# Graph network on one core: propagation started by nine buckets, six row places, and scattered records laid out so that gates load as whole records

## What is computed

```python
# 0: relations. h2 = relu(x @ W1[r] + b1) @ W2[r] for 8 relations
x = ln(x + relu(segment_sum(h2[src, rel_type] * norm, dst) + bias2))
# 1: attention. a = softmax of edge_weight1 within each dst
x = ln(x + elu(segment_sum(x[src] * a[:, None], dst)))
# 2: propagation, twice, over the edges and a loop at each node: r = src, c = dst
w = dinv[r] * dinv[c]                      # dinv = rsqrt(degree)
for _ in range(2):
    y = segment_sum(w[:, None] * y[c], r)  # y = x at first
x = ln(x + y)
# 3: gated messages. gate = silu(edge_attr @ W1.T + b1) @ W2.T + b2 + adapt(src, dst)
agg = segment_sum(gate * x[dst] * (cw * mj)[:, None], src) / clip(segment_sum(mj, src))
x = ln(x + ln(x + agg) * gamma + beta)     # the layer has a layernorm of its own
```

## Time and profile before

| | us |
|---|---|
| three runs: median (lowest to highest) | 6699.7 (6696.94 to 6712.73) |
| the profiled execution, its own time | 6714.21 |
| span of its trace, first to last instruction | 6711.9 |
| busy in the span: PE / DVE / ACT / POOL | 3883.5 / 4094.4 / 2565.0 / 3959.9 |

### The profile page before, as it was taken

How to read it: one execution, slowest core, us unless ns; L and a number is a source line. 1 busy time by engine, 2 the same in 40 slices (tenths; PEclk the granted TensorE clock), 3 DMA queues, 4 the chain that set the end, 5 groups by cost and what they waited for, 6 DMA issues and landing times.

```text
span 6711.9 us, 121393 instructions
## 1 busy us (share of the span) xinstructions
PE 3883.5 (58%) x46613; PEld 2995.6 (45%) x46613; DVE 4094.4 (61%) x7196; ACT 2565.0 (38%) x5259; POOL 3959.9 (59%) x3993
## 2 busy tenths in 40 slices
PE   5445555555555555345555655555565555798775
PEld 5344444333332333224444444444444444787774
DVE  4444444555555556436656666666666667888999
ACT  1111111111111111234445555455455556787664
POOL 2566666666666666665555555555555554236996
PEclk8555555555555555555555555555555556899998
DMA  3455422222222222123333323333333333587886
GB/s 125 157 172 163 136 50 50 48 57 48 49 48 49 48 49 51 30 44 56 58 55 56 59 61 59 56 57 58 57 61 57 58 57 70 159 231 190 190 193 132
DMA packets 1408683, 571.24 MB, mean 85 GB/s; under 512 B 1063555, under 2 KB 1347727, under 8 KB 1407969
## 3 DMA queue, kind: packets, MB, share of 16 engines
q1 hardware_dynamic: 1303201, 452.37, 30.1%
q0 software_dynamic: 104896, 110.96, 7.5%
HBM read 394.81 MB, written 168.16 MB: 84 GB/s over the span
## 4 chain that ended last, share of the span: by engine, by line
PE 22%; another core or an unknown queue 22%; issue 17%; ACT 14%; DVE 14%; DMA 7%; SPq 2%; POOL 2%; DVEq 0%; ACTq 0%; POOLq 0%
DMA rb<-dst_rows 5%; PE ps L1314 4%; PE ps L1527 4%; ACT rb L1674 3%; ACT meta_b L1684 3%; DVE ps L2167 2%; PE ps L1352 2%; ACT meta_a L1606 2%; PE ps L1485 2%; ACT at_table L1704 2%; ACT rb L1704 1%; PE ps L1274 1%; ACT meta_b L1691 1%; PE ps L1302 1%
## 5 line engine op out<-in xcount | busy, mean ns | idle before, releaser
L992 POOL DMA_INDIRECT by_src<-meta_a,row_src x1612 | 1609.0, 998 | 1280.5 <-DVE meta_a L2422 863.7
L981 POOL DMA_INDIRECT ring<-h_table,meta_b x1616 | 1647.4, 1019 | 900.5 <-issue 448.6
L1591 ACT ACTIVATE ring<-ring,meta_b 128x48 f32<-128x48 f32 x1616 | 386.3, 322 | 2103.0 <-DMA ring<-h_table,meta_b 2070.3
L1485 PE MATMUL ps<-dst_i,meta_b 128*128 128x128 bf16 x2450 | 393.4, 292 | 834.1 <-ACT at_table L1704 291.6
L1314 PE MATMUL ps<-ring,WX 128*128 128x48 bf16 x2188 | 437.5, 236 | 554.0 <-DVE row_src L2298 340.7
L2661 DVE TENSOR_TENSOR meta_b<-big,ps 128x1152 bf16<-128x1152 bf16 x546 | 734.6, 1346 | 0.0
L1485 PEld LDWEIGHTS ps<-dst_i,meta_b 128*128 128x128 bf16 x2450 | 228.6, 151 | 1062.4 <-issue 1035.1
L1444 PE MATMUL ps<-WX,meta_b 128*128 128x49 bf16 (+1 forms) x14742 | 594.6, 200 | 77.1 <-issue 43.2
L1314 PEld LDWEIGHTS ps<-ring,WX 128*128 128x128 bf16 x2188 | 361.1, 165 | 581.4 <-DVE row_src L2298 351.8
L1314 PE MATMUL ps<-row_src,WX 128*128 128x48 bf16 x4376 | 490.9, 234 | 220.5 <-issue 218.4
L1444 PEld LDWEIGHTS ps<-WX,meta_b 128*128 128x128 bf16 (+1 forms) x14742 | 574.9, 108 | 93.1 <-issue 46.3
(11 more groups left out here) (353 smaller groups left out, 9089.3 us busy)
## 6 DMA issues: line engine op xcount, KB each, us to landing
by_src<-default SPq DMA_DIRECT2D x44, 1456.0 KB
meta_a<-by_src SPq DMA_DIRECT2D x273, 216.0 KB, 4.3
rb<-lo_rows SPq DMA_DIRECT2D x202, 256.0 KB
rb<-src_rows SPq DMA_DIRECT2D x273, 144.0 KB
rb<-dst_rows SPq DMA_DIRECT2D x273, 144.0 KB
meta_a<-in_attrT SPq DMA_DIRECT2D x402, 80.0 KB
ring<-h_table,meta_b POOLq DMA_INDIRECT x1616
by_src<-meta_a,row_src POOLq DMA_INDIRECT x1612
```

Of the source, the lines that this page charges most:

```text
L981: pool.indirect_dma_start(ring[:, gg % RING, j, 0:width], None, table, bass.IndirectOffsetOnAxis(ap=index(g * GROUP + j), axis=0)) \
L992: pool.indirect_dma_start(by_src, bass.IndirectOffsetOnAxis(ap=row_src[:, t:t + 1], axis=0), rec[:, q % RECS, j, :], None).then_inc(s_sc[q ...
L1485: mm = pe.matmul(bank(5, P, at=i * P), ohS_n[:, a % 3, :, u * TRIO + i], ohK_n[:, a % 2, u * TRIO + i, :], start=True, stop=True)
L1591: scaled = act.activation(row, row, ACT.Copy, scale=meta_b[:, t, M_NORM:M_NORM + 1])
```

## The change

Four edits.

1. *Place of a record.* `place_cells` now works out (128 s + place) x 50 + j: the 50 cells of one place of a source bucket are neighbours, and the 128 places of a cell lie 10,400 bytes apart. The fetches of the fields follow it.
2. *Gates as whole records.* The nine cells of a group then are one run of 9 x 208 = 1,872 bytes on each of the 128 partitions. The load takes the whole records (`gate_n` grows from 48 to 52 floats a record) and is cut where a group passes from one source bucket to the next (`pieces`).
3. *Six row places.* `rb_8` has six slots for the last layer (the three above it served as slots of block stores until then), with semaphores of their own (`s_rowl`). The first six rows are loaded ahead of propagation, before the block loads from the seventh on; row n+6 is loaded right behind the gates of group n, once row n has been turned.
4. *Propagation begun with nine buckets.* DVE works out dinv right after the degrees, scales and splits chunk 0 (nine buckets) and goes into the loop over blocks; the other chunks and the attention of the last four buckets are steps taken in that loop, two before an even block and one before an odd one. ACT answers the exponential at block 19 and the square root at block 27. PE waits in group 0 for the chunk when it comes to the chunk's first bucket.

```diff
@@ place_cells
-                link(dve.tensor_scalar(count_i, dst_i[:, :], 7, 7, ALU.logical_shift_right, ALU.logical_shift_left))
-                link(dve.scalar_tensor_tensor(rows_f, bucket[:, :], float(PER_SRC * P), scratch, ALU.mult, ALU.add))
-                link(dve.tensor_tensor(rows_f, rows_f, count_i, ALU.add))
+                link(dve.tensor_scalar(count_i, dst_i[:, :], 7, None, ALU.logical_shift_right))
+                link(dve.scalar_tensor_tensor(rows_f, bucket[:, :], float(P), scratch, ALU.mult, ALU.add))
+                link(dve.scalar_tensor_tensor(rows_f, rows_f, float(PER_SRC), count_i, ALU.mult, ALU.add))
...
@@ SP: fetches of the fields
-            by_cell = by_src.rearrange("(t p) w -> p t w", p=P)
-            by_bucket = by_src[0:CELLS * P, :].rearrange("(s j p) w -> p s j w", j=PER_SRC, p=P)
+            by_bucket = by_src[0:CELLS * P, :].rearrange("(s p j) w -> p s j w", j=PER_SRC, p=P)
+            after_cells = by_src[CELLS * P:CTILES * P, :].rearrange("(p j) w -> p j w", p=P)
-                by_tile = by_src[0:CELLS * P, :].rearrange("(s j p) w -> j s p w", j=PER_SRC, p=P)
+                by_tile = by_src[0:CELLS * P, :].rearrange("(s p j) w -> j s p w", j=PER_SRC, p=P)
@@ SP: before the block loads, and the last layer
+            def last_rows_load(n):
+                if n >= STORES:
+                    sp.wait_ge(*turned(SGROUPS + n - STORES))
+                    sp.wait_ge(*last_rows_in(n - STORES))
+                sp.dma_start(rb_8[:, n % STORES, :], dst_rows[n * SG:(n + 1) * SG, :].rearrange("(a t) n -> a (t n)", a=1)
+                             .to_broadcast([P, SG * P])).then_inc(s_rowl[n % STORES], 16)
+            sp.wait_ge(*turned(SGROUPS - 1))
+            for n in range(STORES):
+                last_rows_load(n)
             for l in range(LOADS_AHEAD, len(LOADS)):
...
-            for m in range(SGROUPS, 2 * SGROUPS):
-                n = m - SGROUPS
-                sp.wait_ge(*turned(m - 3))
-                sp.wait_ge(s_rowd[m % 3], 16 * (m // 3))
...
-                sp.dma_start(gate_n[:, n % 4, :, :], by_cell[:, n * SG:(n + 1) * SG, 0:FEAT]).then_inc(s_gld[n % 4], 16)
+            for n in range(SGROUPS):
                 if n >= 4:
+                    sp.wait_ge(*gates_in(n - 4))
                 sp.wait_ge(s_msg, SGROUPS + n - 3)
+                for s, j0, j1, at in pieces(n):
+                    sp.dma_start(gate_n[:, n % 4, at:at + j1 - j0, :], by_bucket[:, s, j0:j1, :]).then_inc(s_gld[n % 4], 16)
...
+                if n + STORES < SGROUPS:
+                    last_rows_load(n + STORES)
@@ PE
+                        if k == 0 and c == 0 and d in STARTS:
+                            pe.wait_ge(s_xp, 2 + STARTS.index(d))
...
-                pe.wait_ge(s_xp, 2)
+                pe.wait_ge(s_nacc, N_BUCKETS)
+                pe.wait_ge(s_msg, SGROUPS)
@@ ACT
-                answer("exp", elu[:, 0:LATE[1] - LATE[0], :])
-                answer("sqrt", small[:, 3, LATE[0]:LATE[1]])
                 for b in range(N_BLOCKS):
+                    if b == LATE_EXP_AT:
+                        answer("exp", elu[:, 0:LATE[1] - LATE[0], :])
+                    if b == LATE_ROOT_AT:
+                        answer("sqrt", small[:, 3, LATE[0]:LATE[1]])
@@ DVE
-                late = [attend_chunk(*LATE)]
-                steps(late, 2)
-                inverse_degree()
-                steps(late, 1000)
+                def scaled_chunk(c):
+                    a, b = STARTS[c], CHUNK_ENDS[c]
+                    v, q = V[:, a:b, :], Q[:, a:b, :]
+                    part = [XP[:, a:b, i * FEAT:(i + 1) * FEAT] for i in range(PARTS)]
+                    link(dve.tensor_tensor(v, X[:, a:b, :], dinv[:, a:b][:, :, None].to_broadcast([P, b - a, FEAT]), ALU.mult))
+                    yield
+                    link(dve.tensor_copy(part[0], v))
+                    yield
+                    link(dve.tensor_tensor(q, v, part[0], ALU.subtract))
+                    yield
+                    link(dve.tensor_copy(part[1], q))
+                    yield
+                    link(dve.tensor_tensor(q, q, part[1], ALU.subtract))
+                    yield
+                    dve.tensor_copy(part[2], q).then_inc(s_xp, 1)
+                    yield
...
                 split_multiplicities()
-                link(dve.tensor_tensor(V[:, :, :], X[:, :, :], bc(dinv[:, :]), ALU.mult))
-                for _ in split_steps(V[:, :, :], s_xp):
-                    pass
-                dve.wait_ge(s_xp, 2)
+                inverse_degree()
+                dve.wait_ge(s_dinv, 1)
+                queue = [scaled_chunk(0)]
+                steps(queue, 1000)
+                queue = [scaled_chunk(c) for c in range(1, SUPERS - 1)] + [attend_chunk(*LATE), scaled_chunk(SUPERS - 1)]
                 for b in range(N_BLOCKS):
                     k, c, _, ns, d, own = block_of(b)
+                    if b < STARTS[-1]:
+                        steps(queue, 2 if b % 2 == 0 else 1)
```

More of the change, by code:

```diff
@@ L492, in pieces, with gates_in @@
                 yield d, t0 - d * PER_SRC, t1 - d * PER_SRC, t0 - a0
+        def gates_in(n):
+            return s_gld[n % 4], 16 * sum(len(list(pieces(x))) + (x == SGROUPS - 1 and CTILES > CELLS)
+                                          for x in range(n % 4, n + 1, 4))
         def stored(a):
@@ L497, in stored, with last_rows_in @@
             return BLKW[i] + 16 * sum(len(list(pieces(x))) for x in range(i, a + 1, STORES))
+        def last_rows_in(n):
+            i = n % STORES
+            return s_rowl[i], stored((SGROUPS - 1 - i) // STORES * STORES + i) + 16 * (n // STORES + 1)
+        assert STORES == 6
         SUPERS = len(STARTS)
@@ L588, in build @@
         EXP_IN, ROOT_IN = 3, 14
+        LATE_EXP_AT, LATE_ROOT_AT = 19, 27
         SUMS_AT, NORM_STEPS, ROOT_AT = 5, (13, 19, 25), 21
@@ L913, in _ @@
                 sp.wait_ge(s_blkw[a % STORES], stored(a))
+            for i in range(2):
+                sp.wait_ge(s_roww[i], 48 * len(range(i, N_BUCKETS, 2)))
+            sp.wait_ge(s_padw, 32)
+            def last_rows_load(n):
[7 more added lines that the diff above has]
+                last_rows_load(n)
             for l in range(LOADS_AHEAD, len(LOADS)):
@@ L918, in _ @@
                 block_load(l)
-            for m in range(SGROUPS, 2 * SGROUPS):
-                n = m - SGROUPS
-                sp.wait_ge(*turned(m - 3))
-                sp.wait_ge(s_rowd[m % 3], 16 * (m // 3))
-                if n == 0:
-                    for i in range(2):
-                        sp.wait_ge(s_roww[i], 48 * len(range(i, N_BUCKETS, 2)))
-                    sp.wait_ge(s_padw, 32)
-                sp.dma_start(rb_8[:, m % 3, :], dst_rows[n * SG:(n + 1) * SG, :].rearrange("(a t) n -> a (t n)", a=1)
-                             .to_broadcast([P, SG * P])).then_inc(s_rowd[m % 3], 16)
+            for n in range(SGROUPS):
                 if n >= 4:
-                    sp.wait_ge(s_gld[n % 4], 16 * (n // 4))
+                    sp.wait_ge(*gates_in(n - 4))
                 sp.wait_ge(s_msg, SGROUPS + n - 3)
-                sp.dma_start(gate_n[:, n % 4, :, :], by_cell[:, n * SG:(n + 1) * SG, 0:FEAT]).then_inc(s_gld[n % 4], 16)
+                for s, j0, j1, at in pieces(n):
+                    sp.dma_start(gate_n[:, n % 4, at:at + j1 - j0, :], by_bucket[:, s, j0:j1, :]).then_inc(s_gld[n % 4], 16)
+                if n == SGROUPS - 1 and CTILES > CELLS:
+                    sp.dma_start(gate_n[:, n % 4, SG - (CTILES - CELLS):SG, :], after_cells).then_inc(s_gld[n % 4], 16)
+                if n + STORES < SGROUPS:
+                    last_rows_load(n + STORES)
             sp.wait_ge(s_tab, 1)
@@ L1687, in turn_at_once @@
                 def turn_at_once(m):
-                    act.wait_ge(s_rowd[m % 3], 16 * (m // 3 + 1))
+                    act.wait_ge(*last_rows_in(m - SGROUPS))
                     act.wait_ge(s_ng, taken(m - 3))
-                    act.activation(ohT_8[:, m % 3, :], rb_8[:, m % 3, :], ACT.Abs_reciprocal_sqrt, bias=steep_c[:, 0:1], scale=STEEP,
+                    act.activation(ohT_8[:, m % 3, :], rb_8[:, (m - SGROUPS) % STORES, :], ACT.Abs_reciprocal_sqrt, bias=steep_c[:, 0:1], scale=STEEP,
                                    saturate=False) \
@@ L2785, in last_rows @@
                                 dve.wait_ge(s_nr, m - 3)
[L2786 removed]
+                            dve.wait_ge(*gates_in(n))
                             dve.wait_ge(s_ng, taken(m))
@@ L2830, in sums_of @@
                                           AX_X, ALU.add).then_inc(s_nacc, b - a)
-                link(dve.memset(small[:, 5, :], 0.0))
+                link(dve.memset(small[:, 5, N_BUCKETS:SLOTS], 0.0))
                 split_multiplicities()
-                link(dve.tensor_tensor(V[:, :, :], X[:, :, :], bc(dinv[:, :]), ALU.mult))
-                for _ in split_steps(V[:, :, :], s_xp):
-                    pass
-                dve.wait_ge(s_xp, 2)
```

(7 more changed lines are left out.)

14 lines of the change are left out of this document (7 added, 7 removed).

## The result

| | before | after |
|---|---|---|
| median of the runs, us (12 each) | 6707.6 | 6688.8 |
| lowest to highest | 6694.9 to 6727.4 | 6674.9 to 6705.8 |
| ratio of the times, 95% interval | 1 | 0.9975 [0.9964, 0.9986] |
| profiled execution: span | 6711.9 | 6699.6 |

The change gains 0.25%, 16.8 us by the ratio (9.4 to 24.1), where 28 were forecast. The experiments further down ran in four series. So every kernel is compared inside its own series.

The account below looks back on a forecast made before the run. It took late row loads to keep POOL off its last-layer floor of 1.849 us a group, and PE to bound propagation. 23.2 + 4.5 = 28 us off the median 6699.7 gave 6672, range 6660 to 6684.

Parts of the forecast that it names:

- what it gave 0.22: Whole kernel: the time stays within 0.3% (20 us), about what three runs can't tell from no change; chance 0.22.
- Propagation, 4.5 us: Start of propagation: PE begins 13.6 us sooner, group 0 takes 9.2 us longer; gain about 4.5 us.
- Last layer, 23.2 us: Last layer: with rows in time POOL runs at 1.849 us a group, 502.9 us in place of 526.15.
- price of group 0, 9.2 us: Group 0 of propagation: DVE's added steps set its pace, so it takes some 40 us, 9.2 more than before.
- the prediction's worst bound: Propagation: a loss of 4 us if ACT's answers stall DVE and PE works at 1.2 GHz for most of group 0.
- POOL's queue covers most of that: Start of the last layer: gates 1 to 3 leave only after turns 0 to 2; costed at nothing.
- The rival (a): Last layer: late gates or DVE's pace replace the rows, 1.90 to 1.93 us a group; 0.18, shared with part of another rival.
- a test of the rule on shared ports: Last layer: POOL kept 1.849 us beside a DVE busy 39.17 of 40 us, so blocking does not show.
- Scatter stage, 0: Scatter stage: address step between a cell's places grows from 208 to 10,400 bytes in field fetches; cost put at 0.
- other durations of the two fetches: Scatter stage: changed durations of the 16-byte fetch (3.31 us) and 8-byte fetch (5.89 us) would show the prediction wrong.
- The sum: Whole kernel: 23.2 us from the last layer and 4.5 from propagation, 28 us gained.

Follow-up runs that it names:

- e1_prop: Only propagation begun with nine buckets, added to the kernel before: 5544.18 us against 5543.97, ratio 1.0000 [0.9991, 1.0010].
- e6_gates: The whole change, with gates of groups 0 to 3 asked for ahead of rows 6 to 9: 5502.10 us, ratio 0.9930 to the kernel before.
- e3_records: New place of a record and gates as whole records, three row places, against the kernel before: 5514.08 us, ratio 0.9941 [0.9925, 0.9958].
- e5_rows: Only six row places and their order on SP, old layout and 192-byte pieces, against the kernel before: 5542.85 us, ratio 0.9993.
- e4_noprop: The whole change without the propagation begun with nine buckets: 6788.4 us, ratio 0.9972 [0.9961, 0.9983] to the kernel before.

## Why the prediction came out as it did

The prediction had 28 us and the times say 16.8 (9.4 to 24.1), by their ratio. It held it more likely than not (0.65) that the gain would exceed 0.3%; the measured 0.25% falls into what it gave 0.22. Two terms of its sum were mis-sized: propagation, 4.5 us forecast and 1.3 in the trace, and the last layer, 23.2 forecast and 20.0 in the trace. The end gave 1.7 that nobody forecast. The stages in front, put at nothing, took 11 us in the two traces, or some 6 if the times are compared; that part is within the spread of one execution and stays open.

- *Propagation, 4.5 us.* This step failed in size: 1.3 in the trace (13.2 less 11.9), some 3 in `e1_prop`. The start was right within 0.4, and in group 0 DVE's steps ended when forecast. Wrong was the price of group 0, 9.2 us, which measured 11.9. The prediction counted 15 blocks left at that moment, 9.0 us, and took 1 to 2 off for a lead of PE; 18 blocks were left, 10.6 us, and PE had no lead. It had stood idle for 7.3 us in the group, mostly behind DVE, and had worked at its lower clock for 9.8 us, against 3.4 before. The lower clock stood only in the prediction's worst bound, not in its sum. 1.46 us of DVE's time went to the wait for ACT's square root and some 1.7 to casts of 0.60 us where I had interpolated 0.46.
- *Last layer, 23.2 us.* 20.0 in the trace, with the outcome that was forecast (POOL at its floor) but not by its cause. The prediction gave the six places the lead part ("six groups, 11 us, where it had three") and the lighter queue the second. The runs turn it round: places alone 0, records alone everything. I had read ACT's wait for the rows as the loss. That wait was the route by which POOL came to wait, but the cause was the full queue, which rows and gates share at a DMA share of 0.88: with six places the loss took the other route, by the gates. That the term came near is thus partly luck: by its reasoning the six places were to do most of it, and alone they give nothing. The term was mis-sized by its beginning: gates 1 to 3 leaving after turns 0 to 2, "POOL's queue covers most of that", cost 3.1 us, which `e6_gates` gave back.
- *The rival (a)*, a last layer held by the gates, did not come with the whole change, but its wait is the one of edit 3 alone, at 1.96 us a group where the rival had 1.90 to 1.93. DVE's own pace, 0.04 below POOL's, was enough. And what the prediction took for a test of the rule on shared ports was none: the two DVE instructions of the last layer (L2661, L2788) read one of their inputs from the PSUM tile `ps`, not from SBUF.
- *Scatter stage, 0.* Held, as far as it can be told. The fetches' rows were misread: L814 and L817 are the small fetches of 128 pieces that stand behind the large ones on SP, L813 and L816, and those have 0.39 and 0.32 us, so that a duration there is not the length of its own transfer. The packets tell it: the last of the 6,400 pieces of a bucket started 4.9 us after the issue for the 16-byte fetches and 7.5 us after it for the 8-byte ones, and with the new layout 4.6 and 7.9 (medians; the first of the 8-byte pieces started 0.9 us after the issue before and 1.6 after). So far steps were not dearer, as was concluded. SP's issue of the large 8-byte fetch grew from 0.32 to 0.84 us, one of the prediction's signs of being wrong ("other durations of the two fetches"), without a loss that shows: from SP's issue to DVE's first use of the fields passed some 34 us before and 35 after, 26 to 27 with either layout in the first series, and where the stage is short the layouts don't differ.
- *The end* came 1.7 us sooner after POOL's last subtraction, which was not forecast: DVE is no longer behind POOL with its last one-hots. It takes whole records and six places together: `e3_records`, with three places, did not have this (57.2 us), nor did `e5_rows`, with small pieces (57.4), while `e4_noprop`, with both, had it (55.8).
- *The sum.* In the second series, where the front stages are steady, the same kernel gained 30.3 us (22 to 38). The first series' traces have a dearer last layer with small pieces there (532 to 538 us, not 526), which may be some 6 us of the difference. What share of the missing 11 us in the first measurement was the layout stays open within a few us.

## What to carry to other kernels

When one queue carries several loads, read its DMA share and its packet sizes before giving depth to the load that is late: more slots only hand the lateness to the next load, fewer and larger packets remove it. Idle time that a DMA ends is a loss only if the bounding engine waits too; here ACT waited 110 us for rows beside a POOL without a gap. Work spread into a loop as steps is worth its start less what it adds to the loop, and that includes the stretches in which PE waits and works at its lower clock. A neighbour engine that reads SBUF beside the busy one is no free place for it: here more than half of what it took over came back as longer instructions.

## What the runs showed of the hardware

- The same kernel took 5,544 us in one series and 6,820 in another. Nearly all of it lies where POOL's indirect DMAs run: start to first scatter 2,302 to 2,307 against 2,750 to 2,792 us, scatter stage 2,126 to 2,131 against 2,859 to 2,922; from the last scatter to the degrees 124 to 128 against 133 to 135; from the second group of propagation to the last layer one kernel takes the same within 1 us, and in the last layer within 7. In the short kind four scatters follow each other every 5.1 to 5.5 us (5th to 95th percentile), in the long kind every 5.1 to 11.0. PE, ACT and DVE all stand idle together for 87 us of 3500 to 4000 in the kernel before, and for 19 us in `e1_prop`, and for much of it the profile has no releaser (weight loads of L1485: 189.7 us of "issue"). What it is stays open.
- A DMA piece of 16, 192 and 1,872 bytes occupied a DMA engine for 9, 15 and 78 ns at the median.
- A cast of 432 f32 columns to bf16 on DVE took 0.60 us, as long as a subtraction of that size (0.61), while one of 2,400 columns took 1.41 where the product of that size takes 2.66, and one of 192 columns 0.26 where the subtraction takes 0.35. From 192 to 432 columns the cast grows by 1.4 ns a column, from 192 to 2,400 by 0.5; a subtraction or product grows by 1.0 to 1.1 either way. The quick casts have 4 and 50 rows of 48 columns and the slow one 9. Whether it is the odd number was not tried.
- DVE and POOL stretched each other's instructions to up to twice their length (0.61 to 1.27, 0.76 to 1.53, 0.91 to 1.42).
